# Three edits of order and waiting in a four-network graph kernel: one-hots ahead of places in the sort, gathers that wait for sums, and waits against one number

## The reference

```
# network 0, three layers: messages from both ends of an edge and its weight
m = relu(concat(x[src], x[dst], ew) @ edge_W[l] + edge_b[l])
agg = segment_sum(m, dst)
x = relu(concat(x, agg) @ node_W[l] + node_b[l])
# network 1: agg = segment_sum((h0 @ W_rel[etype])[src], dst), 8 edge types
# network 2: two layers of mean aggregation, segment_sum(h[src], dst) / degree
# network 3, two layers of attention with a softmax over the edges of a source
scores = leaky_relu(s_h[src] + s_t[dst] + s_r[edge_type])      # 500 edge types
w = exp(scores - m[src]) / segment_sum(exp(...), src)
for _ in range(3):
    Z = segment_sum(0.85 * w * Z[dst], src) + 0.15 * h
ent = Z @ W_o[l] + ent
```

## Time and profile before

| what | value |
|---|---|
| median of 3 runs | 14024.08 us (14017.4 to 14031.53) |
| the profiled execution's own time | 14034.0 us |
| its span | 14032.2 us |
| busy in that span: PE, PEld, DVE | 81%, 72%, 77% |
| busy in that span: ACT, POOL | 37%, 18% |
| TensorE's mean granted clock | 0.95 |

### The profile page before, as it was taken

One profiled execution on the slowest core, in us unless ns is written; L12 is line 12 of the kernel. 1 busy time (PEld: TensorE's weight loads), 2 busy tenths in 40 slices (PEclk: granted clock), 3 DMA queues, 4 the chain that ended last, 5 costly groups with the idle time before them and its releaser, 6 DMA issues. The chain is left out here.

```text
span 14032.2 us, 473362 instructions
## 1 busy us (share of the span) xinstructions
PE 11396.0 (81%) x112719; PEld 10086.3 (72%) x112912; DVE 10845.1 (77%) x39414; ACT 5252.1 (37%) x19100; POOL 2474.9 (18%) x7659
## 2 busy tenths in 40 slices
PE   3444488899899689986665779999998779999998
PEld 2444377688788589975554339999998338999998
DVE  5444499688588378886564997779998997779998
ACT  1000022122122122235453237775454236775554
POOL 2777300000000000001110001112222001112222
PEclk9999999899899689999896999999998999999999
DMA  1111166443233011113231553332221553332222
GB/s 50 45 48 45 53 215 214 134 116 116 74 116 116 24 33 40 40 44 81 67 83 48 140 146 101 104 93 73 71 73 53 131 145 103 103 96 73 71 73 62
DMA packets 1206835, 1232.88 MB, mean 88 GB/s; under 512 B 218351, under 2 KB 1042800, under 8 KB 1206106
## 3 DMA queue, kind: packets, MB, share of 16 engines
q1 hardware_dynamic: 1180954, 1228.47, 31.5%
q0 software_dynamic: 25792, 3.35, 0.2%
HBM read 1115.06 MB, written 116.16 MB: 88 GB/s over the span
## 5 line engine op out<-in xcount | busy, mean ns | idle before, releaser
L1672 ACT ACTIVATE msgs<-G,share 128x64 f32<-128x64 f32 x6000 | 1397.1, 316 | 1343.5 <-PE G L1686 1343.5
L976 DVE TENSOR_SCALAR hot<-iota_row,place 128x128 f32<-128x128 f16 (+1 forms) x9000 | 1811.8, 266 | 2.6 <-POOL place L957 1.4
L968 DVE TENSOR_SCALAR hotT<-idx,iota_col 128x512 bf16<-128x512 f16 x4500 | 1315.4, 350 | 614.3 <-PE G L1111 557.7
L1686 PE MATMUL G<-u_b,hotT 128*128 x12000 | 1591.6, 276 | 50.0 <-DVE hotT L1620 50.0
L1053 PE MATMUL G<-table_m,hotT 128*128 x9000 | 1419.5, 248 | 226.3 <-issue 149.7
L1696 PE MATMUL S<-msgs,hot 128*128 128x128 f32 x12000 | 1586.2, 275 | 0.0
L1130 ACT CAST msgs<-G 128x384 bf16<-128x384 f32 x2250 | 1026.2, 481 | 1447.4 <-PE G L1111 1440.8
L1075 DVE TENSOR_REDUCE sums<-G 128x128 f32<-128x384 f32 x2250 | 1247.7, 555 | 376.9 <-PE G L1057 354.9
L1686 PEld LDWEIGHTS G<-u_b,hotT 128*128 128x128 f32 x12000 | 1467.0, 193 | 50.7 <-issue 50.7
L1696 PEld LDWEIGHTS S<-msgs,hot 128*128 128x128 f32 x12000 | 1462.1, 192 | 0.0
L1083 ACT ACTIVATE msgs<-sums 128x128 f32<-128x128 f32 x2250 | 702.6, 312 | 2002.3 <-DVE sums L1075 2002.3
(11 more groups left out here) (322 smaller groups left out, 20714.9 us busy)
## 6 DMA issues: line engine op xcount, KB each, us to landing
idx<-pos_rows SPq DMA_DIRECT2D x6375, 128.0 KB, 2.9
hotT<-hots_d SPq DMA_DIRECT2D x750, 256.0 KB
hots_d<-hotT SPq DMA_DIRECT2D x375, 256.0 KB, 3.1
key_b<-key_rows SPq DMA_DIRECT2D x62, 416.0 KB
ty_b<-type_rows SPq DMA_DIRECT2D x62, 416.0 KB
rows<-rel_rows SPq DMA_DIRECT2D x1500, 6.0 KB
ew_now<-ew_rows_d SPq DMA_DIRECT2D x1125, 3.0 KB
sorted_d<-recs,place POOLq DMA_INDIRECT x806
```

The costliest lines, as they stand in the source:

```text
L968: op = eng.tensor_scalar(hotT[:, c % deep, n], idx[:, c, r], p.col[:, first:first + 1], None, ALU.is_equal)
L976: op = eng.tensor_scalar(hot[:, c % 2, q], p.row16[:], place[:, c % 2, q:q + 1], None, ALU.is_equal)
L1672: op = eng.activation(msgs[:, c % 2, 2 + j // HEADS, j % HEADS * D:(j % HEADS + 1) * D], G[c % 2][1][:, j * D:(j + 1) * D], ACT.Copy, scal ...
L1686: mm = eng.matmul(G[c % 2][b][:, k * W:(k + 1) * W], hotT[:, c % 2, q * P:(q + 1) * P], table[:, ds(dst_at(at, q, 24 * W), W)], start=True ...
```

## The change

In the sort, DVE's step is cut in two functions, `hots` (the one-hots of a group) and `places`, and the program is written so that the one-hots of g+1 stand ahead of the places of g. `hots` of g also waits for `hot` of g-1.

In the message layers, `taken` is handed to `edge_pass` as `freed`, and with it PE's step becomes: gather 0 and gather 1, each after `taken[h]`, then scatter 0 and scatter 1, each after `made[h]`. DVE signals `taken` once at the start for nothing, so ACT waits for one more. Passes of networks 1 and 2 give no `freed` and keep their order.

In the first spread, three semaphores are fresh ones that DVE and ACT count up by 3 (or 4) at the start, so that PE's waits ahead of the scatter compare with t+1, as the one ahead of the gather does. The relation rows signal the same semaphore as the positions (48 in place of 32 per step), for which DVE waits; PE's own wait for them goes, and so does its wait for `made` ahead of the gather.

```
--- before.py
+++ after.py
-                def step(g, h, first):
+                def hots(g, h, first):
+                    if not isinstance(g, int) or g > 0:
+                        after(eng, hot, g)
                     after(eng, rows[h], 48 * ((g - h) // 2 + 1) if first else 24 * (g - h) + 48)
                     if not first:
                         after(eng, lookd, g - 1)
...
                     one_hot_columns(eng, dox[:, h], s.edge_cols[:, 1, ds(g * GRP, GRP)], p).then_inc(hot.h, 1)
+
+                def places(g, h, first):
                     after(eng, lookd, g + 1)
                     after(eng, hot, g + 1)
                     if not first:
...
-                body(eng, step)
+                hots(0, 0, True)
+                hots(1, 1, True)
+                places(0, 0, True)
+                hots(2, 0, False)
+                places(1, 1, True)
+                with eng.Fori(1, S // 2 - 1) as i:
+                    hots(i * 2 + 1, 1, False)
+                    places(i * 2, 0, False)
+                    hots(i * 2 + 2, 0, False)
+                    places(i * 2 + 1, 1, False)
+                hots(S - 1, 1, False)
+                places(S - 2, 0, False)
+                places(S - 1, 1, False)
...
@@ edge_pass
                 eng.nop().then_inc(hots.h, 1)
+                for h in range(H if freed else 0):
+                    eng.nop().then_inc(freed[h].h, 1)
...
                     if scatters:
                         ready(eng, hots, t + 1)
+                    if freed:
+                        for h in range(H if gathers else 0):
+                            ready(eng, freed[h], t + 1)
+                            gather(eng, c, h, at, env).then_inc(gathered[h].h, 1)
+                        for h in range(H if scatters else 0):
+                            ready(eng, made[h], t + 1)
+                            scatter(eng, c, h, was, env).then_inc(scattered[h].h, 1)
+                        return at
...
@@ gnn_layer
-                env["reach"](eng, taken[h], t + 1)
+                env["reach"](eng, taken[h], t + 2)
...
-                  keep="store" if l == 0 else "load")
+                  keep="store" if l == 0 else "load", freed=taken)
...
@@ first_spread
-                                  ).then_inc(rel_in[c].h, 16)
+                                  ).then_inc(idx_in[c].h, 16)
...
-                    arrived(eng, idx_in[c], i0[c], t, c, 32)
+                    arrived(eng, idx_in[c], i0[c], t, c, 48)
...
+                eng.nop().then_inc(folded.h, 1)
+                for _ in range(3):
+                    eng.nop().then_inc(hots.h, 1)
+                    eng.nop().then_inc(folded.h, 1)
...
+                for _ in range(3):
+                    eng.nop().then_inc(made.h, 1)
...
                     reach(eng, turned, tu0, t + 1)
-                    arrived(eng, rel_in[c], r0[c], t, c, 16)
-                    reach(eng, made, m0, t - 3)
...
-                def scatter(t, c):
-                    reach(eng, hots, h0, t + 1)
-                    reach(eng, folded, f0, t)
-                    reach(eng, made, m0, t + 1)
+                def scatter(t, c, now):
+                    reach(eng, hots, 0, now + 1)
+                    reach(eng, folded, 0, now + 1)
+                    reach(eng, made, 0, now + 1)
```

More of the change, by code:

```diff
@@ L884, in src_at, with edge_pass @@
     return (words[0] >> 16).with_bounds(min_val=0, max_val=most)
-def edge_pass(p, s, rows, hot_dt, hot_parts, gather, scatter, vector, scalar, finish, extra=None, keep=None):
+def edge_pass(p, s, rows, hot_dt, hot_parts, gather, scatter, vector, scalar, finish, extra=None, keep=None, freed=None):
     ctx = ExitStack()
@@ L903, in edge_pass @@
         idx_in = [p.fresh("positions") for _ in range(4)]
-        stored = [p.fresh("hots_stored") for _ in range(4)]
+        stored = [p.fresh("hots_stored") for _ in range(4 if keep == "store" else 0)]
         placed, turned, hots = p.fresh("placed"), p.fresh("gather_hot"), p.fresh("scatter_hot")
@@ L1369, in first_spread @@
         idx_in = [p.sem(f"positions_{c}") for c in range(4)]
[L1370 to L1375, removed]
+        turned, hots, made, folded = (p.fresh(x) for x in ("gather_hot", "scatter_hot", "made", "folded"))
+        placed, shared, gathered, scattered, termed, bends, lessed, kept = (p.sem(x) for x in (
+            "placed", "shared", "gathered", "scattered", "termed", "bent", "lessed", "kept"))
+        hots.at, made.at, folded.at = 3, 3, 4
+        i0 = [x.at for x in idx_in]
         tu0, h0, pl0, sh0, sc0, f0, te0, b0, le0, k0 = (x.at for x in (
@@ L1392, in step @@
                                   s.rel_rows[ds(t * 4, 4), at:at + 3 * HEADS, :].rearrange("k r e -> r k e")
-                                  ).then_inc(rel_in[c].h, 16)
+                                  ).then_inc(idx_in[c].h, 16)
                 quarters(eng, step)
                 for c in range(4):
-                    idx_in[c].at += 32 * ((Q - c + 3) // 4)
-                    rel_in[c].at += 16 * ((Q - c + 3) // 4)
+                    idx_in[c].at += 48 * ((Q - c + 3) // 4)
             @block.gpsimd
@@ L1552, in step @@
                     if not isinstance(t, int) or t >= 3:
-                        scatter(t - 3, (c - 3) % 4)
+                        scatter(t - 3, (c - 3) % 4, t)
                 quarters(eng, step)
                 for t in range(Q - 3, Q):
-                    scatter(t, t % 4)
+                    scatter(t, t % 4, t + 3)
                 scattered.at += Q
```

## The result

| | before | changed |
|---|---|---|
| median of 3 runs | 14024.08 us | 13689.98 us (13684.85 to 13693.95) |
| the profiled execution's own time | 14034.0 us | 13693.95 us |

A forecast was written before the change was run, and what follows sets the result against it. Bounds: DVE and PE in series in the sort, DVE in layer 0, PE in layers 1 and 2 and first spread. Gains 62 + 50 + 98 + 12 = 222 us from 14034.0 give 13812, median-adjusted 13802; range 13700 to 13920.

The forecast's parts named there:

- 18.8 + 0.86 + 0.5 = 20.2 us, the soT fully paid: Sort period per group: POOL's own work, `soT` slowing it, and short instructions of the places; from 21.22 us, gaining 62 us.
- The short instructions of the places: Sort: DVE's short instructions in the places, priced like `dox`, would add 0.5 us a group to POOL's time.
- my low end of 19.1: Sort, fastest case per group: POOL's own work of 18.8 us plus one handover gap of 0.3 us.
- 12.5 + 2.65: Sort, POOL's issue time per group: 13 issues of 0.96 us, plus excess of issues slowed beside DVE instructions.
- That rival, which I gave 0.10: Sort, also called the full handover: POOL gets no slower than today, 19.1 us a group, 13735 us in all; chance 0.10.
- its end of 75: Layer 0: upper end of the forecast gain, 0.20 us a step, 75 us; the forecast itself was 50.
- The floor of 2.32 us: Layer 0 step on DVE: 2.27 us with an unhindered pair of sums plus 0.05 for the loop's turn; from 2.454.
- 0.13 of the 0.21 us: Layers 1 and 2: share of an ordinary step's loss taken as regained, mean over four steps; times 750, 98 us.
- The rival that PE's sequencer leaves nothing: Message layers: PE's sequencer already limits layers 1 and 2, losing their 98 us and half of layer 0's 50; 13925 us, chance 0.12.
- First spread: First spread: removed register instructions and waits save 0.08 us at each loop turn, 15 us at most; 12 taken.

The follow-up runs named there:

- order alone: Changed kernel with gathers waiting for ACT's messages (`made`) again, both gathers still ahead of both scatters: 13908.09 us, against 13789.09 for the changed kernel at that chip speed.
- the six nops: Changed kernel with six empty DVE instructions behind DVE's work in the sort: 13792.52 us; layers 1 and 2 took 805.1 and 803.0 us.
- 16 steps: Changed kernel with 16 steps instead of 4 in PE's loop of the message layers and network 1 and 2 passes: 13573.26 us, against 13789.09 on that chip.
- four buffers: Changed kernel with four buffers and semaphores instead of two for the sort's places and records: 13782.06 us.

## Why the prediction was wrong, point by point

**Sort: the failed step.** What goes and what is late next were right: the order took PE off the path, and POOL holds the sort without a gap. The step "18.8 + 0.86 + 0.5 = 20.2 us, the soT fully paid" is wrong in both additions. soT adds nothing: it holds an issue that starts in it, but that issue then gets through inside `tyT`, so it lasts 2.86 us with 0.98 us of soT ahead of `tyT` and 3.03 us with 0.44. The mean excess of the long issue over 0.96 us is 1.9 us a group in both kernels, and soT a second time made it shorter (2.34 us). The short instructions of the places cost nothing either; issues beside them take 0.96 us. The same sum also has no term for the gap between two groups, 0.30 us, which its low end has; with it the forecast would have been 20.5 us and farther off.

What is left is my low end of 19.1 less 0.2: 14.92 us of issues (I had 12.5 + 2.65) and 13 gaps of 0.305. The 0.2 us is `dox`. It lengthened an issue to 1.47 us in every group before (61 issues of the trace) and does so in every second group now (32); in the others the issue beside `dox` takes 0.96 us. That is 0.23 us a group, 14 us in 61. That rival, which I gave 0.10, was the case; its 67 us, and 14 more beyond it, are 81 of the 112 us that the forecast lacks.

**Layer 0: a term mis-sized.** 84 us in place of 50, above its end of 75. The wait of the second sum went, as said. The floor of 2.32 us was 0.08 too high, 30 us in 375 steps. 0.05 of it is the turn of the loop, which costs DVE nothing once it never waits (every step is 2.238 us, the turn's too). 0.03 is that I took the pair of sums by its length (1.17 less 1.05) and not from start to start: 1.09 us in the step that I used and 0.94 now. The 84 us are no sharper than the place of the code allows: in kernels with the old code of this layer it took 918.7, 925.6 and 938.3 us.

**Layers 1 and 2: right** in mechanism, and for the reason given: the wait for the sums takes ACT off PE's path (order alone gives nothing). That the size hits 98 us exactly is luck: with the same edit these layers gained 113 us with the messages' edit alone and 112 with the six nops, and no row stood behind 0.13 of the 0.21 us. Ordinary steps of 1.96 to 2.04 and a turn of 2.69 us (the median of its steps) were forecast as 1.97 and 2.65. The rival that PE's sequencer leaves nothing is out; at the turn PE does stand, 0.72 us, and 16 steps give most of that back. **First spread: right**, 13 us for 12, and at the turn, as said.

**The range** ended at 13700. The full handover (13735) with layer 0 at its end (25 us more) is 13710; the 14 us beyond the sort's end (`dox`) and the 9 beyond layer 0's were in no term, though 19.1 was called the low end of a bound.

## What to carry to other kernels

A price for an instruction that another engine runs beside it is read from a row in which it was paid, and prices of neighbours that meet the same instruction are not simply added: here the second was hidden in the first, and a third came due in every second group only. A step's floor is added up from start to start of its instructions, without their lengths and without a price for the turn that nobody has seen on a busy engine. After a wait is removed, look at the turn of the loop: here it was worth 216 us more, on a chip where the change itself gives 477.

## What the runs showed of the hardware

- The same kernel took 14030 us on one chip and 14266 to 14275 us on two others, all of it in one stage, where DVE waits 14.03 and not 10.05 us. PE's rows of the lookups last 9.86 us on both; DVE starts 4.0 us behind the last of them on the slower chip and 0.04 us on the faster. A change that hides this wait is worth 334 us on the one and 477 us on the other.
- In some groups of the changed kernel there, PE's instructions came 0.7, 1.4 or 2.1 us apart for some 40 us, with no wait in the profile, and for a while DVE's came 0.7 us apart too. What starves them is open; records that land late are not it, since four buffers changed nothing (20.57 against 20.48 us a group).
- A POOL indirect DMA takes 0.96 us to issue, 1.06 beside `scalar_tensor_tensor` with two SBUF inputs, 1.47 or 0.96 beside `dox`, depending on where they meet, 2.9 to 3.0 beside soT and `tyT`, and 4.7 to 5.1 with three more comparisons of `tyT`. With soT alone beside it for 1.43 us it was not done. Where soT was made twice, the issues that began in the midst of `tyT` took 0.96 us, and `tyT` 2.56 in place of 2.32.
- Six empty instructions of DVE far ahead of a loop made two layers 14 us shorter (805.1 and 803.0 us in place of 813.4 and 808.8).
